# Attention weights times values in float32 on TensorE, with the output transposed, in place of a bf16 split on VectorE

## The chip, the cores and the metric

The kernel runs on all 8 NeuronCores of one Trainium2 chip, each core on its own half of one of four sequences, without exchange between the cores. The metric is the device time in microseconds of the slowest core. The median of two runs of the kernel before is 8694.8 us (8690.62 to 8698.98).

## What is computed

A layer normalisation and attention with 16 heads of 64, then a second layer normalisation and a feed-forward part with quantised weights, both with a residual addition. The change touches the attention alone:

```python
h = jnp.einsum('bse,end->bsnd', x, proj_weight)        # x after layer norm
q = jnp.einsum('bsnd,ndh->bsnh', h, attn_weight)
scores = jnp.einsum('bsnh,brnh->bsnr', q, h) / head_dim
w = jax.nn.softmax(scores, axis=-1)
v = jnp.einsum('brnd,ndh->brnh', h, value_weight)
attn_out = jnp.einsum('bsnr,brnh->bsnh', w, v).reshape(b, s, -1)
return attn_out @ out_w.T + out_b
```

Batch 4, 4096 positions, width 1024. A core holds one sequence of 4096 keys and computes 2048 of its queries.

## The kernel before

**Order of the work.** Every engine has one queue, written in the order of the `@blk` pieces, with semaphores between the queues; there is no scheduler. First the feed-forward weights are quantised (to about 600 us). Then, for each of two groups of four head pairs, `emit_hbuild` computes h for all 4096 positions (about 550 us each), and `emit_attention` runs once for each head pair (8 times, p = 0 to 7). The feed-forward part follows from about 5980 us on.

**float32 by halves.** Where float32 accuracy is wanted, a float32 tile is split into a bf16 tile "hi" and the bf16 rest "lo", and TensorE adds three bf16 products in PSUM: hi hi, hi lo, lo hi. Splitting takes VectorE a cast, a drain (it waits until its own writes are done) and a subtract.

**A head pair** (L554 to L873). Two heads of 64 lie in partitions 0 to 63 and 64 to 127. First the *value build* (L595 to L629): for 32 chunks of 128 keys (`NRC` = 32) TensorE computes v for both heads with six small matmuls, and VectorE writes it to `vA` and `vB` as 64 columns hi, a column of ones, and 64 columns lo. Then four *blocks* (`sc_i`) of 512 queries.

**A block.** TensorE computes the queries (L647), VectorE splits them and takes their largest absolute value (L658 to L661), a DMA issued by POOL brings that to one row (L669), and after some small steps a bias for the exponential lies in `cbias` (L707, semaphore `g_cb`).

The *loop* has 32 rounds over the key chunks (L737 to L755). In round rc TensorE issues the scores of the chunk, three matmuls of 512 columns for each head (L744, keys stationary, 64 rows of the array for each head), and after them the value matmuls of the chunk before (`emit_av`). ScalarE takes the exponentials of both heads into `w32`, float32, two slots for each head (L767). VectorE splits them into `w_hi` and `w_lo` (L777, L779). In `emit_av` the weights are stationary: for each head and each 128 queries a matmul of `w_hi` with 129 columns of v and one of `w_lo` with 65 (L720, L724), 16 in all. The column of ones gives the sum of the weights, so the result lies with queries on partitions and its sum beside it:

```python
te.matmul(pav[:, pofs:pofs + 129], w_hi[:, wofs + st * 128:wofs + (st + 1) * 128],
          vb[:, rc * 132:rc * 132 + 129], start=(rc == 0 and st % 2 == 0), stop=False)
```

The *tail*: VectorE takes eight reciprocals of the sums (L792), and for each head and 128 queries multiplies and adds the two parts (L801, L804). TensorE transposes the result (L817), VectorE splits it (L827, L829), TensorE multiplies it with the output weights (L848, 8 groups of three matmuls into `pb_q` and `pb_o` in turn), and VectorE adds each group to the residual `x_tm` (L872). The next block's query matmuls wait for the last of these additions (`v_res`), and its first score matmul for `g_cb`.

## Time and profile before

| | |
|---|---|
| profiled execution | 8699.6 us, span of the slowest core (2) 8698.0 us |
| spans of the 8 cores | 8682.4 to 8698.0 us |
| mean granted TensorE clock | 0.758 to 0.762 of full speed |
| TensorE matmuls busy | 4127.8 us, 47% of the span |
| VectorE busy | 5227.4 us, 60% |
| ScalarE busy | 1586.3 us, 18% |
| POOL busy | 67.7 us, 1% |

The profile is of one execution, so sums are made against its own 8699.6 us. A busy share is an average over stages; busy times of matmuls hold their latency, and matmuls overlap each other. A row of the timeline gives the start, the duration, engine, line and operation, output and inputs, and in brackets the idle time before it with the engine that ended it (DVEq and PEq are the sequencers of VectorE and TensorE, where a drain ends). "x2" are two instructions merged. The clock is a share of 2.4 GHz; 0.50 is 1.2 GHz.

### The profile page before, as it was taken

Reading aid. Unit: us, or ns where it says so; the run is one execution under the profiler, and the core shown is the slowest. Engines: PE = TensorE matmul, PEld = TensorE weight load, DVE = VectorE, ACT = ScalarE, POOL = GpSimd, SP = SyncE. Lnnn points to the kernel's source line nnn. Section 1 sums busy time; section 2 is a strip of 40 time slices with the busy share of each in tenths; the row PEclk is TensorE's granted clock in tenths of the full one; section 3 lists DMA queues with packets and bytes.
Section 4 is the critical chain, followed back from the end, with each engine's and each line's share of the span. In section 5 each row is a group of like instructions: output and inputs, shape, how many; then the busy total and the mean of one; then the engine's idle time right before and its main releaser. Section 6 shows DMA issues by size and latency. Waiting matters only on the chain.

```text
span 8698.0 us, 121004 instructions; the slowest of 8 cores (8682.4 to 8698.0 us)
## 1 busy us (share of the span) xinstructions
PE 4127.8 (47%) x38438; PEld 2597.9 (30%) x38438; DVE 5227.4 (60%) x12623; ACT 1586.3 (18%) x2602; POOL 67.7 (1%) x102
## 2 busy tenths in 40 slices
PE   0016645455555555645555454555454353353453
PEld 0015523223222225532222222323232232232232
DVE  5666667777677776667777777665434435434434
ACT  0000023233233331013233232321000000000000
POOL 0000000000000000000000000000000000000000
PEclk9996778788788887778888887876666665566666
DMA  8741000000000001100000000002333343343343
GB/s 271 234 137 35 30 6 1 4 1 1 4 1 1 1 9 41 35 11 1 4 1 1 4 1 1 1 1 47 75 87 66 75 90 67 67 99 66 78 85 70
DMA packets 835921, 394.33 MB, mean 45 GB/s; under 512 B 803427, under 2 KB 803555, under 8 KB 829156
## 3 DMA queue, kind: packets, MB, share of 16 engines
q1 hardware_dynamic: 827044, 353.00, 17.1%
q0 software_dynamic: 8256, 33.58, 1.0%
q8 instruction: 325, 5.32, 0.3%
q14 instruction: 296, 2.42, 0.1%
HBM read 352.95 MB, written 33.55 MB: 44 GB/s over the span
## 4 chain that ended last, share of the span: by engine, by line
DVE 47%; PE 26%; issue 12%; DMA 7%; DVEq 7%; ACT 1%; SPq 0%; ACTq 0%; POOLq 0%; POOL 0%
DVE w_lo L779 15%; DVE w_hi L777 9%; PE pb_av L462 6%; PE pf_d L1368 2%; PE pf_u L1195 2%; PE pf_g L1190 2%; PE pf_d L1195 2%; PE pf_d L1190 2%; DMA f_wd<-wdq 2%; PE pb_s L744 2%; DVE ln_lo L479 2%; DVE ln_hi L477 2%; PE pb_o L848 1%; DVE f_guq L1341 1%; PE pb_q L848 1%
## 5 line engine op out<-in xcount | busy, mean ns | idle before, releaser
L767 ACT ACTIVATE w<-pb_s,cbias 128x512 f32<-128x512 f32 x2048 | 1297.4, 684 | 1531.9 <-PE pb_s L744 1515.0
L779 DVE TENSOR_TENSOR w_lo<-w,w_hi 128x512 bf16<-128x512 f32 x2048 | 1417.9, 692 | 159.4 <-issue 6.8
L777 DVE CAST w_hi<-w 128x512 bf16<-128x512 f32 x2048 | 875.8, 428 | 561.2 <-issue 356.8
L720 PE MATMUL pb_av<-vA,w_hi 128*128 128x129 bf16 x4096 | 517.2, 226 | 1148.3 <-DVEq L782 1148.0
L720 PEld LDWEIGHTS pb_av<-vA,w_hi 128*128 128x128 bf16 x4096 | 384.0, 100 | 1646.7 <-issue 1646.7
L1368 PE MATMUL pf_d<-f_guq,f_wd 128*128 128x256 bf16 x2048 | 297.7, 319 | 634.4 <-DVE f_guq L1341 543.8
L720 PE MATMUL pb_av<-vB,w_hi 128*128 128x129 bf16 x4096 | 518.2, 226 | 0.0
L744 PE MATMUL pb_s<-q_hi,h_hi 64*128 64x512 bf16 x2048 | 461.4, 411 | 103.0 <-ACT w L767 72.1
L724 PE MATMUL pb_av<-vA,w_lo 128*128 128x65 bf16 x4096 | 491.9, 198 | 0.0
L724 PE MATMUL pb_av<-vB,w_lo 128*128 128x65 bf16 x4096 | 490.7, 198 | 0.0
L744 PE MATMUL pb_s<-q_lo,h_hi 64*128 64x512 bf16 x2048 | 455.9, 405 | 0.0
L744 PE MATMUL pb_s<-q_hi,h_lo 64*128 64x512 bf16 x2048 | 454.6, 404 | 0.0
L1368 PEld LDWEIGHTS pf_d<-f_guq,f_wd 128*128 128x128 bf16 x2048 | 230.5, 114 | 703.2 <-issue 645.3
L720 PEld LDWEIGHTS pb_av<-vB,w_hi 128*128 128x128 bf16 x4096 | 387.1, 101 | 0.0
L724 PEld LDWEIGHTS pb_av<-vB,w_lo 128*128 128x128 bf16 x4096 | 381.5, 100 | 0.0
L724 PEld LDWEIGHTS pb_av<-vA,w_lo 128*128 128x128 bf16 x4096 | 378.5, 100 | 0.0
L1190 PE MATMUL pf_g<-f_xqf,f_wg 128*128 128x256 bf16 x1024 | 202.8, 365 | 277.1 <-DVEq L1223 262.3
L1190 PE MATMUL pf_d<-f_xqf,f_wg 128*128 128x256 bf16 x1024 | 202.7, 364 | 273.8 <-DVEq L1223 273.8
L1233 ACT ACTIVATE f_si<-f_gr 128x256 f32<-128x256 f32 x256 | 106.6, 417 | 1232.2 <-DVEq L1223 1232.2
L462 PE MATMUL pb_av<-ln_hi,pw_hi 128*128 128x128 bf16 x2048 | 215.6, 268 | 239.8 <-DVE h_lo L492 234.2
L1210 DVE TENSOR_TENSOR f_gr<-pf_g,f_fb 128x256 f32<-128x256 f32 x128 | 54.4, 425 | 454.3 <-PE pf_u L1195 454.3
L1210 DVE TENSOR_TENSOR f_gr<-pf_d,f_fb 128x256 f32<-128x256 f32 x128 | 54.4, 425 | 452.0 <-PE pf_d L1195 448.1
(222 smaller groups left out, 6841.7 us busy)
## 6 DMA issues: line engine op xcount, KB each, us to landing
f_wg<-wgq SPq DMA_DIRECT2D x256, 256.0 KB, 3.3
f_wu<-wuq SPq DMA_DIRECT2D x256, 256.0 KB, 3.9
f_wd<-wdq SPq DMA_DIRECT2D x64, 1024.0 KB, 8.0
wraw<-wgT SPq DMA_DIRECT2D x16, 2048.0 KB, 10.2
wraw<-wuT SPq DMA_DIRECT2D x16, 2048.0 KB, 9.8
wraw<-wdT SPq DMA_DIRECT2D x64, 512.0 KB, 4.4
xa<-x_full SPq DMA_DIRECT2D x64, 512.0 KB, 3.5
x_tm<-x_full SPq DMA_DIRECT2D x16, 512.0 KB, 12.9
```

The lines of the kernel that those rows point to most:

```text
L462: last = te.matmul(pp[:, 0:128], wop[:, ic * 512 + lc * 128:ic * 512 + (lc + 1) * 128], rop[:, ic * 128:(ic + 1) * 128], start=first, stop ...
L477: v.tensor_copy(ln_hi[:, ib * 128:(ib + 1) * 128], src)
L479: v_ls.inc(v.tensor_tensor(ln_lo[:, ib * 128:(ib + 1) * 128], src, ln_hi[:, ib * 128:(ib + 1) * 128], ALU.subtract))
L720: te.matmul(pav[:, pofs:pofs + 129], w_hi[:, wofs + st * 128:wofs + (st + 1) * 128], vb[:, rc * 132:rc * 132 + 129], start=(rc == 0 and st ...
L724: last = te.matmul(pav[:, pofs:pofs + 65], w_lo[:, wofs + st * 128:wofs + (st + 1) * 128], vb[:, rc * 132:rc * 132 + 65], start=False, sto ...
L744: last = te.matmul(pb_s[hidx][:, 0:512], kop[hidx * 64:hidx * 64 + 64, hofs + rc * 128:hofs + (rc + 1) * 128], qop[hidx * 64:hidx * 64 + 6 ...
L767: a_e.inc(sc.activation(w32[:, slot:slot + 512], pb_s[hidx][:, 0:512], AFT.Exp, bias=cbias[:, hidx:hidx + 1], scale=1.0 / 64))
L777: v.tensor_copy(w_hi[:, slot:slot + 512], w32[:, slot:slot + 512])
L779: v.tensor_tensor(w_lo[:, slot:slot + 512], w32[:, slot:slot + 512], w_hi[:, slot:slot + 512], ALU.subtract)
L1190: te.matmul(pg[:, 0:FSC], f_wg[:, buf + ic * 128:buf + (ic + 1) * 128], f_xqf[:, ic * FSC:(ic + 1) * FSC], start=(ic == 0), stop=(ic == 7))
L1195: last = te.matmul(pu[:, 0:FSC], f_wu[:, buf + ic * 128:buf + (ic + 1) * 128], f_xqf[:, ic * FSC:(ic + 1) * FSC], start=(ic == 0), stop=(i ...
L1368: last = te.matmul(pd[:, 0:FSC], f_wd[:, (ec % 2) * 4096 + ic * 128:(ec % 2) * 4096 + (ic + 1) * 128], f_guq[:, ic * FSC:(ic + 1) * FSC], ...
```

## The change

The weights are no longer split. The value matmul is turned round: v is stationary (float32, 64 columns and the column of ones, so 65) and the float32 weights are the moving operand, 512 queries at once. There is one matmul for each head and round, waiting for ScalarE itself (`a_e`). Its output has the head's 64 dimensions on partitions 0 to 63 and the sums in row 64, queries along the free axis. This form is the one the output projection wants, so the transposes go; but the sums now lie in one row, so their reciprocals are taken as rows of 512, split into hi and lo, and spread over the partitions by one-row matmuls with a row of ones into `pb_av[0]` and `pb_av[1]`. The second head's result lies in partitions 0 to 63 and is moved to 64 to 127 by a DMA that POOL issues. The projection writes to `pb_av[0]` and `pb_av[1]` instead of `pb_q` and `pb_o`, so the next block's query matmuls wait for `g_cb` instead of `v_res`, and the first score matmul waits no longer for `g_cb`. ScalarE waits for the value matmuls two rounds back instead of VectorE's split. `vA` and `vB` become float32 tiles of 66 columns for each chunk, written by a copy and a memset.

```diff
+                        v.tensor_copy(vb[:, rc * 66:rc * 66 + 64], pav[:, 0:64])
+                        v.memset(vb[:, rc * 66 + 64:rc * 66 + 65], 1.0)
-                        v.tensor_copy(vb[:, rc * 132:rc * 132 + 64], pav[:, 0:64])
-                        v.memset(vb[:, rc * 132 + 64:rc * 132 + 65], 1.0)
-                        v.drain()
-                        v.tensor_tensor(vb[:, rc * 132 + 65:rc * 132 + 129],
-                                        pav[:, 0:64],
-                                        vb[:, rc * 132:rc * 132 + 64], ALU.subtract)
                     v_ve.inc(v.drain())
...
                     v_ve.w(te, bvve + NRC)
                     t_s.w(te)
-                    v_res.w(te)
+                    g_cb.w(te)
...
                     def emit_av(rc):
-                        v_w.w(te, bvw + 2 * rc + 2)
                         for hidx in range(2):
+                            a_e.w(te, bae + 2 * rc + hidx + 1)
+                            if rc == 0:
+                                v_af.w(te, bvaf)
                             wofs = (2 * (rc % 2) + hidx) * 512
                             vb = [vA, vB][hidx]
-                            last = None
-                            for st in range(4):
...
+                            last = te.matmul(
+                                pb_av[2 + hidx][0:65, 0:512],
+                                vb[:, rc * 66:rc * 66 + 65],
+                                w32[:, wofs:wofs + 512],
+                                start=(rc == 0), stop=(rc == NRC - 1))
                         t_av.inc(last)
 
-                    g_cb.w(te, bgcb + 1)
-                    v_nm.w(te, bvnm)
-                    v_af.w(te, bvaf)
+                    a_e.w(te, bae)
...
                     t_av.w(v, btav + NRC)
                     t_at.w(v, btat)
                     for hidx in range(2):
...
+                        v.reciprocal(rr_t[64:65, hidx * 512:(hidx + 1) * 512],
+                                     pb_av[2 + hidx][64:65, 0:512])
                     v.drain()
...
+                    for hidx in range(2):
+                        te.matmul(pb_av[hidx][:, 0:512],
+                                  onesb_t[64:65, 0:128],
+                                  rhib[64:65, hidx * 1024:hidx * 1024 + 512],
+                                  start=True, stop=False, tile_position=(64, 0))
+                        t_at.inc(te.matmul(
...
+                    v.tensor_copy(fbA_t[:], pb_av[0][:, 0:512])
...
+                    v.tensor_tensor(attn_tm[0:64, 0:512], pb_av[2][0:64, 0:512],
+                                    fbA_t[0:64, 0:512], ALU.mult)
...
+                @blk.gpsimd
+                def _(gp):
+                    v_af.w(gp, bvaf + 4)
+                    d_pk.inc(gp.dma_start(out=attn_tm[64:128, 0:512],
+                                          in_=attnB_s[0:64, 0:512]), 16)
+
+                @blk.vector
+                def _(v):
+                    d_pk.w(v)
+                    v.tensor_copy(attn_hi[:], attn_tm[:])
+                    v.drain()
+                    v.tensor_tensor(attn_lo[:], attn_tm[:], attn_hi[:], ALU.subtract)
+                    v_as.inc(v.drain())
...
-                            pp = [pb_q, pb_o][eh]
+                            pp = [pb_av[0], pb_av[1]][eh]
```

TensorE in the loop, before, from the last score matmul of a round on. `pb_av` is the accumulator, `vA` the values of the first head, `w_hi` and `w_lo` the halves of the weights:

```order
L744 MATMUL pb_s<-q_hi,h_lo 128x512
L720 MATMUL pb_av<-vA,w_hi 128x129 [waits v_w]
L724 MATMUL pb_av<-vA,w_lo 128x65
L720 MATMUL pb_av<-vA,w_hi 128x129
L724 MATMUL pb_av<-vA,w_lo 128x65
```

The pair of rows L720 and L724 stands eight times in a row, four times for each head, behind one wait for VectorE. The same place after the change (line numbers of the changed kernel):

```order
L735 MATMUL pb_s<-q_hi,h_lo 128x512
L718 MATMUL pb_av<-w,vA 65x512 [waits a_e]
L718 MATMUL pb_av<-w,vB 65x512 [waits a_e]
L735 MATMUL pb_s<-q_hi,h_hi 128x512 [waits a_e]
L735 MATMUL pb_s<-q_lo,h_hi 128x512
L735 MATMUL pb_s<-q_hi,h_lo 128x512
```

Two instructions have taken the place of sixteen, each waits for ScalarE alone, and the order of scores and values is the same.

VectorE from the end of a loop to the residual, before:

```order
L779 TENSOR_TENSOR w_lo<-w,w_hi 128x512
L784 UNCONDITIONAL_BRANCH
L792 RECIPROCAL sums_t<-pb_av 128x1 [waits t_av]
L792 RECIPROCAL sums_t<-pb_av 128x1 x7
L801 TENSOR_SCALAR attn_tm<-pb_av,sums_t 128x64
L804 SCALAR_TENSOR_TENSOR attn_tm<-pb_av,sums_t,attn_tm 128x64
```

The last two rows stand eight times; then come four casts and subtracts of 128 columns, each pair behind a transpose. After the change, from behind the reciprocals on:

```order
L772 CAST rhib<-rr_t 1x512 x2
L776 TENSOR_TENSOR rhib<-rr_t,rhib 1x512 x2
L797 UNCONDITIONAL_BRANCH
L801 COPY fbA_t<-pb_av 128x512 [waits t_at]
L804 COPY fbB_t<-pb_av 128x512 [waits t_at]
L806 TENSOR_TENSOR attn_tm<-pb_av,fbA_t 64x512
L809 TENSOR_TENSOR attnB_s<-pb_av,fbB_t 64x512
L819 UNCONDITIONAL_BRANCH
L822 CAST attn_hi<-attn_tm 128x512 [waits d_pk]
L824 TENSOR_TENSOR attn_lo<-attn_tm,attn_hi 128x512
```

`fbA_t` and `fbB_t` hold the spread reciprocals, `d_pk` is the new DMA. The piece has fewer and longer instructions, and waits once for TensorE's spreading and once for the DMA. The split of `attn_tm` and the projection behind it now wait for all 512 queries, where before each 128 went on by themselves.

## Rows read from the trace of the kernel before

**Rows 1.** Timeline of VectorE (DVE), a round of the loop.

```profile
4003.15 0.43 DVE L777 CAST w_hi<-w 128x512 bf16<-128x512 f32 x1 [0.19 <-issue]
4003.65 0.69 DVE L779 TENSOR_TENSOR w_lo<-w,w_hi 128x512 bf16<-128x512 f32 x1
...
4005.91 0.43 DVE L777 CAST w_hi<-w 128x512 bf16<-128x512 f32 x1 [0.18 <-issue]
```

**Rows 2.** Timeline of TensorE (PE), the same round.

```profile
4002.55 0.40 PE L744 MATMUL pb_s<-q_hi,h_hi 64*128 64x512 bf16 x2
...
4002.77 0.39 PE L744 MATMUL pb_s<-q_lo,h_hi 64*128 64x512 bf16 x2
...
4004.52 0.22 PE L720 MATMUL pb_av<-vA,w_hi 128*128 128x129 bf16 x1 [1.14 <-DVEq L782]
...
4005.18 0.19 PE L724 MATMUL pb_av<-vB,w_lo 128*128 128x65 bf16 x1
...
4005.30 0.40 PE L744 MATMUL pb_s<-q_hi,h_hi 64*128 64x512 bf16 x2
```

**Rows 3.** Timeline of ScalarE (ACT), the same round.

```profile
4003.52 1.26 ACT L767 ACTIVATE w<-pb_s,cbias 128x512 f32<-128x512 f32 x2 [1.50 <-PE pb_s L744]
```

**Rows 4.** Stretches: length, busy us and count of PE, PEld, DVE, ACT, POOL, clock, DMA, GB/s.

```profile
3960.20:3970.00 9.80, 6.87 (x46) 3.05 (x47) 4.48 (x8) 4.22 (x6) 0.00 (x0) 0.52 0.00 0
...
3976.50:4055.00 78.50, 45.11 (x619) 27.07 (x617) 62.72 (x112) 35.11 (x56) 0.00 (x0) 1.00 0.01 1
...
684.00:689.00 5.00, 3.92 (x48) 3.29 (x45) 2.42 (x7) 0.29 (x1) 0.00 (x0) 0.81 0.40 105
```

**Rows 5.** Timeline of VectorE, the first reciprocals of three blocks in a row.

```profile
3932.57 0.62 DVE L792 RECIPROCAL sums_t<-pb_av 128x1 f32<-128x1 f32 x8 [1.28 <-PE pb_av L724]
...
4055.97 0.63 DVE L792 RECIPROCAL sums_t<-pb_av 128x1 f32<-128x1 f32 x8 [1.53 <-PE pb_av L724]
...
4178.43 0.62 DVE L792 RECIPROCAL sums_t<-pb_av 128x1 f32<-128x1 f32 x8 [1.33 <-PE pb_av L724]
```

**Rows 6.** Timeline of TensorE, first projection matmul, first scores, round 1, next block.

```profile
3941.83 0.63 PE L848 MATMUL pb_q<-ow_hi,attn_hi 128*128 128x512 bf16 x1
...
3960.18 0.61 PE L744 MATMUL pb_s<-q_hi,h_hi 64*128 64x512 bf16 x2 [0.97 <-DVE cbias L707]
...
3965.26 0.63 PE L744 MATMUL pb_s<-q_hi,h_lo 64*128 64x512 bf16 x1
...
4083.46 0.61 PE L744 MATMUL pb_s<-q_hi,h_hi 64*128 64x512 bf16 x2 [0.97 <-DVE cbias L707]
```

**Rows 7.** Timeline of TensorE, float32 transposes of 128 columns in the h build.

```profile
3303.22 0.27 PE L447 MATMUL pb_o<-id32s,lnt 128*128 128x128 f32 x1
3303.32 0.38 PE L447 MATMUL pb_s<-id32s,lnt 128*128 128x128 f32 x2
```

**Rows 8.** Groups of instructions by line: count, busy us, mean ns, idle before.

```profile
L872 DVE TENSOR_TENSOR x_tm<-x_tm,pb_o 128x512 f32<-128x512 f32 x128 | 88.1, 689 | 63.8 <-PE pb_o L848 36.7 <-PE pb_o L857 26.6 <-issue 0.5
...
L1281 DVE RECIPROCAL f_trw<-f_trw 1x256 f32<-1x256 f32 x8 | 13.9, 1741 | 0.7 <-issue 0.2
```

**Rows 9.** Timeline of VectorE, behind the small DMA of POOL.

```profile
3957.00 0.21 DVE L675 TENSOR_REDUCE csc<-mq_row 1x1 f32<-1x64 f32 x1 [2.72 <-DMA mq_row<-mq_t]
```

**Rows 10.** DMA issues: count, KB each, median us from issue to landing.

```profile
y<-x_tm POOLq DMA_DIRECT2D x16, 512.0 KB, 3.3
...
mq_row<-mq_t POOLq DMA_DIRECT2D x32, 0.5 KB, 1.9
```

**Rows 11.** Timeline of VectorE, one key chunk of the value build.

```profile
4345.92 0.23 DVE L623 CAST vA<-pb_av 128x64 bf16<-128x64 f32 x1 [0.19 <-issue]
...
4346.37 0.21 DVE L623 CAST vB<-pb_av 128x64 bf16<-128x64 f32 x1
...
4347.08 0.23 DVE L623 CAST vA<-pb_av 128x64 bf16<-128x64 f32 x1 [0.18 <-issue]
```

**Rows 12.** Timeline of VectorE, first step of a block's queries.

```profile
3952.22 0.69 DVE L658 CAST q_hi<-pb_q 128x512 bf16<-128x512 f32 x1 [1.20 <-PE pb_q L647]
```

More of the change, by code:

```diff
@@ L146, in _ @@
         v.memset(ones_row[:], 1.0)
+        v.memset(onesb_t[:], 1.0)
         v.memset(sc_t[:, 0:1], 0.75)
@@ L772, in _ @@
                 def _(v):
-                    for rc in range(NRC):
-                        for hidx in range(2):
-                            a_e.w(v, bae + 2 * rc + hidx + 1)
-                            slot = (2 * (rc % 2) + hidx) * 512
-                            v.tensor_copy(w_hi[:, slot:slot + 512], w32[:, slot:slot + 512])
-                            v.drain()
-                            v.tensor_tensor(w_lo[:, slot:slot + 512],
-                                            w32[:, slot:slot + 512],
-                                            w_hi[:, slot:slot + 512], ALU.subtract)
-                            v_w.inc(v.drain())
-                @blk.vector
-                def _(v):
                     t_av.w(v, btav + NRC)
@@ L811, in _ @@
                     v_nm.w(te, bvnm + 1)
-                    a_e.w(te, bae + 64)
-                    for st in range(4):
-                        tid = btat + st
-                        if st >= 2:
-                            v_af.w(te, bvaf + st - 1)
-                        t_at.inc(te.transpose(
-                            pb_s[st % 2][:, 0:128],
-                            attn_tm[:, st * 128:(st + 1) * 128], id32[:]))
+                    v_res.w(te, bvres)
+                    for hidx in range(2):
+                        te.matmul(pb_av[hidx][:, 0:512],
+                                  onesb_t[64:65, 0:128],
+                                  rhib[64:65, hidx * 1024:hidx * 1024 + 512],
+                                  start=True, stop=False, tile_position=(64, 0))
+                        t_at.inc(te.matmul(
+                            pb_av[hidx][:, 0:512],
+                            onesb_t[64:65, 0:128],
+                            rhib[64:65, hidx * 1024 + 512:hidx * 1024 + 1024],
+                            start=False, stop=True, tile_position=(64, 0)))
@@ L821, in _ @@
                 @blk.vector
                 def _(v):
+                    t_at.w(v, btat + 1)
                     t_op.w(v, btop)
-                    for st in range(4):
-                        t_at.w(v, btat + st + 1)
-                        src = pb_s[st % 2][:, 0:128]
-                        v.tensor_copy(attn_hi[:, st * 128:(st + 1) * 128], src)
-                        v.drain()
-                        v_af.inc(v.tensor_tensor(
-                            attn_lo[:, st * 128:(st + 1) * 128], src,
-                            attn_hi[:, st * 128:(st + 1) * 128], ALU.subtract))
+                    v.tensor_copy(fbA_t[:], pb_av[0][:, 0:512])
```

86 lines of the change are left out of this document (39 added, 47 removed).

## The prediction

> **What bounds the kernel now.** I read the granted clock of all cores first (0.758 to 0.762, spans within 16 us, so one core stands for all), then the busy time in 100 us stretches, which showed where the 32 attention blocks lie, then the timeline of one block, engine by engine. A block is 512 query rows of one head pair: a loop of 32 rounds over the keys, and a tail that normalises, projects and adds.
>
> In the loop VectorE sets the pace. From one CAST of the first head to the next is 4005.91 - 4003.15 = 2.76 us [rows 1], and it spends them on two casts (0.43) and two subtracts (0.69), each started by a semaphore. TensorE's score matmuls start 0.22 us apart, and the two heads go side by side (x2) [rows 2]: 3 x 0.215 = 0.65 us a round. The 16 value matmuls take 0.66 us (4004.52 to 5.18), and before them TensorE idles 1.14 us for VectorE's drain. ScalarE does two exponentials in 1.26 us and idles 1.50 [rows 3]. So nothing but the split of the weights into two bf16 halves holds a round at 2.76.
>
> The whole loop, from the first score matmul to the first reciprocal, takes 4055.97 - 3960.18 = 95.8 us in one block and 4178.43 - 4083.46 = 95.0 in the next [rows 5, 6]. I use 95. The way from that reciprocal to the output projection is 3941.83 - 3932.57 = 9.3 us, and to the next loop 27.6 us; here work goes from engine to engine one step at a time. In the loop proper TensorE is granted 1.00 (2.4 GHz), in its first 10 us 0.52, which is almost all at 1.2 GHz [rows 4].
>
> **The loop after.** The VectorE split goes. TensorE takes the float32 weights as moving operand, in two matmuls of 512 columns a round. What an ordinary float32 matmul costs is not in the trace, since all float32 ones there are transposes. Low bound: the rate of bf16, 0.215 us per 512 columns [rows 2]. The float32 transposes stand about 0.11 us apart for 128 columns [rows 7], so 0.44 per 512. High bound: four products, each at that transpose rate, 1.74. Between them I take four products at the bf16 rate, 4 x 0.215 = 0.86 us: this kernel itself builds a nearly float32 product of three bf16 products (it leaves out low times low), and the nearest matmuls with 512 columns are those score matmuls. The other end of the transposes, 0.44, would be two products and is a rival below.
>
> The Trainium skill (FP8 and Floating Point Precision, TensorE Precision Notes) says that a true float32 product is four passes through the array; by it the price of a matmul would be the same 0.86 us, and no run before this one shows it.
>
> A round is then 0.65 + 2 x 0.86 = 2.37, and I add 0.07 us at each change between score and value matmuls: from the last value matmul to the next score matmul 0.12 us pass (4005.18 to 5.30), of which its 65 columns are about 0.03 [rows 2]. That gives 2.50 us, with TensorE busy without a gap. It is the bound if the exponentials keep up: they start 0.97 us after the first score matmul and are done at 2.23 (4002.55, 4003.52 + 1.26) [rows 2, 3], and their word reaches TensorE some 0.14 later, at 2.37. The value matmuls of the round before are only done at about 2.43. So the cover is thin, 0.06 us, and whatever makes the value matmuls cheaper brings little below 2.4 unless the heads stagger.
>
> The start of a loop is at half clock. The last score matmul of round 1 starts 5.1 us after the first of round 0 [rows 6], ends its columns at 5.5, and then a pair of value matmuls costs 3.4 us: 8.9; scores of round 2 end at 10.2. Here the clock comes up [rows 4], and the second pair ends at about 12.0. Thirty rounds remain: 30 x 2.50 = 75.0, and 0.4 for the last drain and semaphore. Loop: 87.4 us, **-7.6 us x 32 = -243**.
>
> **The tail after.** On VectorE two reciprocals of 1 x 512 stand where eight of 128 x 1 stood. The only long reciprocal in the trace takes 1741 ns for 256 elements [rows 8], so 3.4 us each, 6.8. (If it cost as much as any operation of 512 elements, 0.69 [rows 8], the block would be 5.4 us shorter, 173 us in all. That is the low bound.) Two casts of 0.43 and two subtracts of 0.69 with drains: 9.2 us after the first reciprocal. Then TensorE's four one-row matmuls at half clock, 0.43 to the second and 0.63 for it [rows 6], with a semaphore: the first factor is there at 10.5. Two copies and two products on VectorE, 0.69 and a drain each: 13.6. The DMA through POOL moves 128 KB between partitions. A tiny one keeps VectorE waiting 2.72 us [rows 9], 1.9 of it from issue to landing, where 512 KB take 3.3 [rows 10]. So 0.8 us are the way to the issue, and with 2.15 for the landing I take 2.95; bounds 2.7 and 0.8 + 3.3 = 4.1 (1.15 x 32 = 37 us more). At 16.6 VectorE casts and subtracts 512 columns, 17.9, and the projection starts at 18.2 instead of 9.3: +8.9. The projection and the residual additions stay, only in other PSUM banks. What is queued behind the new DMA wait on VectorE is the residual, and behind TensorE's wait the projection: nothing can fill the gap.
>
> Two waits get lighter. The first score matmul no longer waits for the bias copy, of which 0.97 us are seen [rows 6]; about 0.85 come back, hidden by nothing, because the exponential table is loaded only after the scores. Sum per block 8.9 - 0.85 = 8.05, **x 32 = +258**. The query matmul no longer waits for the last residual addition, since the projection has left its bank: VectorE idles 1.20 us for it [rows 12], 1.1 come back in the 24 blocks that have another block of the same pair before them, **-26**.
>
> **The value build.** Per key chunk VectorE did cast, memset, drain, subtract for each head, 4347.08 - 4345.92 = 1.16 us, at half clock and with TensorE ahead of it. Without the drain and subtract a head goes from 0.45 (4345.92 to 6.37) to about 0.24: 0.66 in all with the 0.18 of semaphore [rows 11]. -0.5 us x 32 chunks x 8 pairs = **-128**. Bounds: 0 if the ping-pong with TensorE takes over, -150 at best.
>
> **Sum** against the profiled execution's 8699.6 us: -243 + 258 - 26 - 128 = -139, 8561. The median of the shown runs is 4.8 us lower, so **8557 us**, 1.6% less. The change wins in the loop, pays it back in the tail, and what stays is the value build. I give this case its own range of 8470 to 8650, a round of 2.42 to 2.60 being 30 x 32 x 0.18 = 173 us of it.
>
> **Rival 1, the clock (slower).** TensorE goes from half idle to streaming all of the loop, on eight cores. In the stretch at 684 us, in a phase of dense matmuls, the granted clock is 0.81 [rows 4], while the loops show 1.00 with TensorE idle 1.14 of 2.76 us. If the loops run at 0.81, the streaming part 2.37 becomes 2.91 and a round 3.05; the loop is 12.6 + 91.5 + 0.2 = 104.3, +9.3 x 32 = +298 instead of -243, so 9098 us. It decides once the loop gains less than the (258 - 154)/32 = 3.2 us a block that the rest loses: 91.8 us, a round of (91.8 - 12.4)/30 = 2.65, which a mean clock of 0.94 already brings (2.37/0.94 + 0.14). For it: the 0.81 was granted to matmuls that paused between rounds. Against it: value matmuls with 65 of 128 columns leave half of the array unused.
>
> The Trainium skill (TensorE: Matmul & The Clock Gate, Part 1) warns of a limiter that takes a die to 13/16 of the clock within about 5 to 20 us once a third core of it runs dense matmuls. By that rule all loops here would run at 0.81, which is this rival's 9098 us; the trace agrees only in that a grant of 0.81 exists.
>
> **Rival 2, dearer float32.** At 1.74 a matmul a round is 4.27 and the time near 10350 us; a weight load left uncovered ahead of each of the eight products, some 0.07 us, gives 3.06 and 9100. For it: float32 transposes run at half the bf16 rate. Against: bf16 loads are fully covered in the loop.
>
> **Rival 3, cheaper float32.** With two products, 0.44 a matmul, the exponentials bind: the heads stagger, six score matmuls in a row and 0.87 of values, about 2.25 with changes. Loop 79.5, -15.5 x 32 = -496, 8304 us.
>
> **Chances.** Forecast 0.47, rival 1 0.30, rival 2 0.12, rival 3 0.11. Faster by over 2% (under 8521, about what a measurement can tell from no change): all of rival 3 and 0.14 of the forecast, 0.25. Slower by over 2%: rivals 1 and 2, 0.42. Within: 0.33. The range, 8300 to 9150, leaves out the dear end of rival 2, the low edge of rival 3 and a little of rival 1.
>
> **What would show it.** Right: two value matmuls a round, their passes about 0.215 us apart, round 2.50 with TensorE never idle for a releaser; first reciprocal to projection 18 us, half of it reciprocals; value chunks 0.66 apart. Wrong: granted clock under 1.00 late in the loop (rival 1), passes dearer than 0.215 at full clock (2), a round under 2.4 with TensorE waiting for ACT (3), or a reciprocal row far from 3.4 us.

## The result and the profile after

The changed kernel takes 8582.8 us (median) against 8700.0 us of the kernel before in the same session. The ratio is 0.9865, with a 95% interval of 0.9852 to 0.9879: 1.35% faster, which is inside the 2% that I called no change, and 26 us from the 8557 us of the prediction. The profiled execution took 8585.86 us, 113.7 less than the 8699.6 of the one before. In three of the nine executions of this kernel one die or both show a lower mean clock and the time is 8773 to 8877 us, which is longer than the kernel before took in any; such executions (of some variants up to 6% longer) are left out of every comparison here.

The page of the kernel after, busy times and one of the costliest groups (line, engine, operation, output and inputs, count, busy time and mean, idle time before and what ended it):

```profile
span 8584.3 us, 85041 instructions; the slowest of 8 cores (8553.9 to 8584.3 us)
PE 5086.0 (59%) x26150; PEld 2252.7 (26%) x26150; DVE 2983.5 (35%) x7376; ACT 1588.9 (19%) x2602; POOL 83.1 (1%) x134
...
L768 DVE RECIPROCAL rr_t<-pb_av 1x512 f32<-1x512 f32 x64 | 210.1, 3320 | 2848.3 <-PE pb_av L718 2848.3
```

VectorE's busy time falls from 5227.4 to 2983.5 us and its idle time now stands ahead of the reciprocals: it does nothing in the loops. TensorE's rises from 4127.8 to 5086.0. That 2244 us of VectorE work are gone and 114 us of time is the first thing to take from this page: the work that went lay partly beside TensorE's, and TensorE's own grew into the room.

TensorE in one round at full clock, core 1 (start, duration, operation; x2 is one for each head), answering to [rows 2]:

```profile
2230.04 0.40 PE L735 MATMUL pb_s<-q_hi,h_hi 64*128 64x512 bf16 x2
...
2230.49 0.39 PE L735 MATMUL pb_s<-q_hi,h_lo 64*128 64x512 bf16 x2
2230.80 1.07 PE L718 MATMUL pb_av<-w,vA 128*65 128x512 f32 x2
2231.71 1.02 PE L718 MATMUL pb_av<-w,vB 128*65 128x512 f32 x2
2232.66 0.40 PE L735 MATMUL pb_s<-q_hi,h_hi 64*128 64x512 bf16 x2
```

No row has an idle time in brackets. The round is 2232.66 - 2230.04 = 2.62 us, and so it is in every block. For the scores x2 is one matmul for each head; a float32 matmul shows as two records, so there x2 is one head. Taken singly, inside one kind of matmul, the records stand 0.429 us apart, so a float32 matmul of 512 columns takes 0.858 us, four times 0.215. The ends of a round are dearer than I had them. Last score start to first value start is 2230.80 - 2230.49 = 0.31, where the columns of the score matmul are 0.215: 0.10 for the change. Behind the last value matmul 2231.71 + 2 x 0.43 would be 2232.57, and the next score matmul starts at 2232.66: 0.10 again. Head A takes 2231.71 - 2230.80 = 0.91, 0.05 over 0.86. So 0.65 + 1.72 + 0.25 = 2.62.

The stretch at full clock (busy us of PE, PEld, DVE, ACT, POOL, each with its count, then granted clock, DMA share, GB/s), and ScalarE in the round, answering to [rows 4] and [rows 3]:

```profile
2190.00:2270.00 80.00, 80.00 (x304) 21.21 (x303) 0.00 (x0) 38.06 (x60) 0.00 (x0) 1.00 0.00 1
```

```profile
2231.01 1.27 ACT L759 ACTIVATE w<-pb_s,cbias 128x512 f32<-128x512 f32 x2 [1.35 <-PE pb_s L735]
```

TensorE is busy for 80 of 80 us at a granted clock of 1.00. The exponentials are done at 2232.28, 0.38 us before TensorE's next score matmul; 0.14 of that is the way of their word, which leaves 0.24. Up to the end of the value matmuls' columns at 2232.57 the cover is 0.15, where I had priced 0.06.

The start of a block:

```profile
2305.14 0.62 PE L735 MATMUL pb_s<-q_hi,h_hi 64*128 64x512 bf16 x2
...
2310.78 1.93 PE L718 MATMUL pb_av<-w,vA 128*65 128x512 f32 x2
2312.55 1.02 PE L718 MATMUL pb_av<-w,vB 128*65 128x512 f32 x2
2313.50 0.40 PE L735 MATMUL pb_s<-q_hi,h_hi 64*128 64x512 bf16 x2
```

Head A's float32 matmul takes 1.77 us (at half clock), head B's 0.95: the clock came up inside the first pair of value matmuls, on the mean of the 32 blocks 8.2 us after the first score matmul, where before it was 10.75. In this execution the loops of all eight cores show 0.50 at the start and 1.00 from then on, and no other level.

VectorE in the tail, answering to [rows 5] and [rows 8], and TensorE's two releases in it:

```profile
2394.13 6.57 DVE L768 RECIPROCAL rr_t<-pb_av 1x512 f32<-1x512 f32 x2 [88.59 <-PE pb_av L718]
2400.77 0.75 DVE L772 CAST rhib<-rr_t 1x512 bf16<-1x512 f32 x2
...
2404.70 0.69 DVE L801 COPY fbA_t<-pb_av 128x512 f32<-128x512 f32 x1 [1.46 <-PE pb_av L791]
...
2407.19 0.68 DVE L809 TENSOR_TENSOR attnB_s<-pb_av,fbB_t 64x512 f32<-64x512 f32 x1
2410.80 0.43 DVE L822 CAST attn_hi<-attn_tm 128x512 bf16<-128x512 f32 x1 [2.92 <-DMA attn_tm<-attnB_s]
```

```profile
2412.28 0.59 PE L843 MATMUL pb_av<-ow_hi,attn_hi 128*128 128x512 bf16 x1 [6.90 <-DVEq L825]
```

From the first reciprocal to the projection 2412.28 - 2394.13 = 18.15 us, with the two long pieces where the prediction put them: 6.6 of reciprocals and 2.92 of waiting for the DMA.

The value build, one chunk 2160.85 - 2160.28 = 0.57 us where it was 1.16 [rows 11]:

```profile
2160.28 0.23 DVE L626 COPY vA<-pb_av 128x64 f32<-128x64 f32 x1 [0.19 <-PE pb_av L612]
...
2160.85 0.23 DVE L626 COPY vA<-pb_av 128x64 f32<-128x64 f32 x1 [0.19 <-PE pb_av L612]
```

Means over the blocks of each trace, in us, x being how often the stretch occurs:

| | before | after | difference | x | sum | predicted |
|---|---|---|---|---|---|---|
| first score matmul to first reciprocal | 95.23 | 89.39 | -5.84 | 32 | -186.6 | -243 |
| first reciprocal to projection | 9.02 | 17.83 | +8.81 | 32 | +282.2 | +285 |
| split of the queries to first score matmul | 7.95 | 7.12 | -0.83 | 32 | -26.5 | -27 |
| last residual to next query split, in a pair (1.89 and 0.85 in most) | 2.00 | 0.92 | -1.08 | 24 | -25.9 | -26 |
| the same with the value build between | 44.63 | 25.04 | -19.6 | 6 | -117.6 | -96 |
| start of the program to the first query split | 1157.2 | 1139.7 | -17.5 | 1 | -17.5 | -16 |
| last residual to query split, with the h build between | 584.4 | 566.8 | -17.6 | 1 | -17.6 | -16 |
| projection and residual additions | 9.87 | 9.57 | -0.30 | 32 | -9.6 | 0 |
| behind the last block | 2734.7 | 2740.1 | +5.4 | 1 | +5.4 | 0 |

Each of the eight value builds lies in one of the three rows that name a build or the start: together -153 us, predicted -128. The sum of all rows is -113.7 us, as the two spans of 8698.0 and 8584.3 us have it.

### The profile page after: what moved, and what is told of

It is laid out like the page before. It is cut to its first block, busy times and chain, and to the rows that moved or that the text cites. A ratio compares the mean times of both kernels' runs of the same rounds, so it can differ in the third digit from the quotient of the medians.

```text
span 8584.3 us, 85041 instructions; the slowest of 8 cores (8553.9 to 8584.3 us)
## 1 busy us (share of the span) xinstructions
PE 5086.0 (59%) x26150; PEld 2252.7 (26%) x26150; DVE 2983.5 (35%) x7376; ACT 1588.9 (19%) x2602; POOL 83.1 (1%) x134
## 3 DMA queue, kind: packets, MB, share of 16 engines
q1 hardware_dynamic: 827044, 353.00, 17.6%
## 4 chain that ended last, share of the span: by engine, by line
PE 55%; DVE 23%; DMA 8%; issue 7%; DVEq 6%; ACT 0%; SPq 0%; POOLq 0%; ACTq 0%; POOL 0%
PE pb_av L718 23%; PE pb_s L735 10%; PE pb_av L464 6%; PE pb_av L843 3%; PE pf_d L1364 2%; PE pf_u L1191 2%; PE pf_g L1186 2%; PE pf_d L1191 2%; PE pf_d L1186 2%; DMA f_wd<-wdq 2%; DVE ln_lo L481 2%; DVE ln_hi L479 2%; DVE f_guq L1337 1%; DVE f_gr L1328 1%; DVE rr_t L768 1%
## 5 line engine op out<-in xcount | busy, mean ns | idle before, releaser
L768 DVE RECIPROCAL rr_t<-pb_av 1x512 f32<-1x512 f32 x64 | 210.1, 3320 | 2848.3 <-PE pb_av L718 2848.3
L718 PE MATMUL pb_av<-w,vA 128*65 128x512 f32 x2048 | 1125.2, 632 | 0.0
L718 PE MATMUL pb_av<-w,vB 128*65 128x512 f32 x2048 | 1055.4, 597 | 0.0
L718 PEld LDWEIGHTS pb_av<-w,vB 128*65 128x65 f32 x2048 | 287.2, 140 | 617.6 <-issue 617.6
L735 PEld LDWEIGHTS pb_s<-q_hi,h_hi 64*128 64x128 bf16 x2048 | 109.4, 93 | 888.3 <-issue 886.0
L718 PEld LDWEIGHTS pb_av<-w,vA 128*65 128x65 f32 x2048 | 203.4, 138 | 454.1 <-issue 454.1
L843 PE MATMUL pb_av<-ow_hi,attn_hi 128*128 128x512 bf16 x256 | 124.3, 486 | 232.8 <-DVEq L825 221.5
L464 PEld LDWEIGHTS pb_av<-ln_hi,pw_hi 128*128 128x128 bf16 x2048 | 178.1, 125 | 253.4 <-issue 253.4
L1191 PE MATMUL pf_u<-f_xqf,f_wu 128*128 128x256 bf16 x1024 | 232.8, 404 | 0.0
L867 DVE TENSOR_TENSOR x_tm<-x_tm,pb_av 128x512 f32<-128x512 f32 x256 | 176.3, 689 | 160.9 <-PE pb_av L843 101.1
```

Source lines behind the costliest of these rows:

```text
L464: last = te.matmul(pp[:, 0:128], wop[:, ic * 512 + lc * 128:ic * 512 + (lc + 1) * 128], rop[:, ic * 128:(ic + 1) * 128], start=first, stop ...
L718: last = te.matmul(pb_av[2 + hidx][0:65, 0:512], vb[:, rc * 66:rc * 66 + 65], w32[:, wofs:wofs + 512], start=(rc == 0), stop=(rc == NRC - 1))
L735: last = te.matmul(pb_s[hidx][:, 0:512], kop[hidx * 64:hidx * 64 + 64, hofs + rc * 128:hofs + (rc + 1) * 128], qop[hidx * 64:hidx * 64 + 6 ...
L768: v.reciprocal(rr_t[64:65, hidx * 512:(hidx + 1) * 512], pb_av[2 + hidx][64:65, 0:512])
L843: last = te.matmul(pp[:, 0:512], a[:, st * 128:(st + 1) * 128], o[:, eh * 512:(eh + 1) * 512], start=first, stop=stop)
L867: v_res.inc(v.tensor_tensor(xd, xd, pp[:, 0:512], ALU.add))
```

## The experiments

My theory went on record with each run: the loop is bound by TensorE's streaming, four passes to a float32 matmul and a price for each change between the two kinds of matmul; the tail is a chain in which reciprocals and DMA are paid in full. The rivals: the clock, the exponentials, and the orientation of the product as the true cause.

**e_stat: the weights stay the stationary operand, in float32.** This undoes the transposed output and the new tail, and keeps the missing split.

```diff
-                            last = te.matmul(
-                                pb_av[2 + hidx][0:65, 0:512],
-                                vb[:, rc * 66:rc * 66 + 65],
-                                w32[:, wofs:wofs + 512],
+                            for st in range(4):
+                                last = te.matmul(
+                                    pb_av[2 * hidx + st // 2][
+                                        :, (st % 2) * 129:(st % 2) * 129 + 65],
+                                    w32[:, wofs + st * 128:wofs + (st + 1) * 128],
+                                    vb[:, rc * 66:rc * 66 + 65],
...
-                        v.reciprocal(rr_t[64:65, hidx * 512:(hidx + 1) * 512],
-                                     pb_av[2 + hidx][64:65, 0:512])
+                            v.reciprocal(sums_t[:, 4 * hidx + st:4 * hidx + st + 1],
+                                         pav[:, pofs + 64:pofs + 65])
```

> The changed kernel, but the float32 weights are the stationary operand again (128x128) and the float32 values the moving one (65 columns), with the old tail (reciprocals of 128x1, one multiply each, transposes, no spreading, no DMA). Theory A, the weight load sets the price: the float32 loads of 65 columns took 0.13 to 0.14 us in the changed kernel and are covered by passes of 0.43; loads of 128 columns cannot be covered by passes of 65 columns, so two loads a matmul of 0.11 to 0.14 us make 1.7 to 2.2 us a round for eight matmuls against 1.72 now; round 2.6 to 3.1. Theory B, only the streamed columns count: four passes of 65 columns are 0.11 us a matmul, 0.87 a round, and the exponentials bind at about 2.2. Both: the tail from the first reciprocal to the projection falls from 17.8 to about 6.5 us (9.0 of the kernel before, less eight operations of 0.36), -360 us in 32 blocks. Time: A 8220 to 8720, B about 7800 us.

Measured: 10533.5 us, ratio 1.2108 (1.2090 to 1.2126). TensorE's matmuls and its weight loads in one round, and a stretch of the loop:

```profile
3101.82 1.97 PE L719 MATMUL pb_av<-vA,w 128*128 128x65 f32 x8
3103.58 1.91 PE L719 MATMUL pb_av<-vB,w 128*128 128x65 f32 x8
3105.42 0.62 PE L738 MATMUL pb_s<-q_hi,h_hi 64*128 64x512 bf16 x2
```

```profile
3101.81 1.78 PEld L719 LDWEIGHTS pb_av<-vA,w 128*128 128x128 f32 x8 [0.84 <-issue]
```

```profile
3100.00:3150.00 50.00, 50.00 (x222) 37.79 (x221) 0.00 (x0) 12.64 (x20) 0.00 (x0) 0.50 0.00 1
```

The granted clock is 0.50 through every loop: it never rises, in none of the 32, on none of the eight cores. The eight value matmuls are 16 records, 0.213 us apart (with the changes at both ends 3105.42 - 3101.82 = 3.60 us), in two equal parts: a load starts, the matmul starts 0.106 us behind it, and the next load 0.107 us behind that. At 1.2 GHz the 130 columns of two passes are 0.108 us, and the load takes about the same; nothing of it is covered. The round is 5.01 us, the loop 163.1, +73.7 x 32 = +2360; the old tail is back (4.81 us to the projection), -417. Together +1943, and the profiled executions differ by +1953. Theory A had the load right (0.107 us, expected 0.11 to 0.14) and the clock wrong, so neither of the two times, 7800 and up to 8720 us, came near.

What follows: with weights stationary half of TensorE's time in a value product is loading. The Trainium skill (TensorE: Matmul & The Clock Gate, Weight-path perf modes) says that the fast weight load works for 128 columns and not for float32; the trace agrees, the load taking as long as the 130 columns that follow it. The same matmuls in bf16 (the run e_stat_bf1 below), at the same 1.2 GHz, start 0.054 us apart, which is their 65 columns alone:

```profile
2300.05 0.40 PE L719 MATMUL pb_av<-vA,w 128*128 128x65 bf16 x4
2300.26 0.41 PE L719 MATMUL pb_av<-vB,w 128*128 128x65 bf16 x4
```

By my estimate the round of e_stat would at 2.4 GHz be half of 5.01, 2.5 us, no worse than the 2.62 of the changed kernel. So the uncovered loads alone do not make this kernel slow; the clock that did not rise does. Why it stays down here, with TensorE shown busy in all of the stretch, no run settles.

**e_nodma: VectorE writes head B's product to partitions 64 to 127 itself,** and the DMA and its wait go.

```diff
-                    v.tensor_tensor(attnB_s[0:64, 0:512], pb_av[3][0:64, 0:512],
+                    v.tensor_tensor(attn_tm[64:128, 0:512], pb_av[3][0:64, 0:512],
...
-                    d_pk.inc(gp.dma_start(out=attn_tm[64:128, 0:512],
-                                          in_=attnB_s[0:64, 0:512]), 16)
...
-                    d_pk.w(v)
```

> The changed kernel, but VectorE writes the second head's product straight to partitions 64 to 127, so the DMA through POOL and its wait go. Theory, the tail is a chain with nothing beside it: first reciprocal to projection falls from 17.8 by the 2.95 us that I gave the DMA to 14.9, 32 times, -94 us: 8492. Rival: part of the DMA was hidden, or a write that changes the partitions is slower than 0.69 us: under 50 us less.

Measured: 8504.7 to 8512.9 us, ratio 0.9783 (0.9763 to 0.9802). VectorE, core 3:

```profile
2381.36 0.68 DVE L809 TENSOR_TENSOR attn_tm<-pb_av,fbB_t 64x512 f32<-64x512 f32 x1
2382.16 0.43 DVE L815 CAST attn_hi<-attn_tm 128x512 bf16<-128x512 f32 x1
```

The product that shifts partitions takes 0.68 us like the other, and the cast follows 0.80 after it, where in the changed kernel it stood 3.61 later (2407.19 to 2410.80). First reciprocal to projection 15.02 instead of 17.83, -2.81 x 32 = -90. Some of that is given back elsewhere in the block (loop +0.15, projection and residual +0.26), and the profiled executions differ by 81. The DMA wait was on the path in full, and needless.

**e_norecip: a copy in place of each reciprocal.** The softmax's division is left out.

```diff
-                        v.reciprocal(rr_t[64:65, hidx * 512:(hidx + 1) * 512],
+                        v.tensor_copy(rr_t[64:65, hidx * 512:(hidx + 1) * 512],
```

> The changed kernel with the two reciprocals of 1x512 replaced by copies of the same form, so the result is not divided by the sums. Theory: a copy takes 0.43 to 0.69 us in place of 3.32, so 5.3 to 5.8 us less in each tail, -168 to -185 us: about 8410. Rival: the time of such a row lies in reading one partition of PSUM, not in the reciprocal, and the copies take as long: no change, 8586.

Measured: 8425.9 us, ratio 0.9685 (0.9666 to 0.9704), so 157 us less than after. Core 0:

```profile
2348.36 1.29 DVE L768 COPY rr_t<-pb_av 1x512 f32<-1x512 f32 x2 [89.59 <-PE pb_av L718]
```

Two copies take 1.29 us, two reciprocals 6.57. First reciprocal to projection is 12.26, -5.57 x 32 = -178. The loop is 0.26 longer and the projection chain 0.35, together +19: what follows a shorter pause is not quite the same afterwards. So the two rows of 512 sums cost 5.3 us a block more than copies of the same form, and this is the largest part of what the transposed output did to the tail.

**e_bf1: weights and values in bf16, without low parts.** Same instructions, other types, so the value matmul is one pass and not four.

```diff
-        vA = asb("vA", [128, NRC * 66], F32)
-        vB = asb("vB", [128, NRC * 66], F32)
+        vA = asb("vA", [128, NRC * 66], BF16)
+        vB = asb("vB", [128, NRC * 66], BF16)
...
-                     bsb("w32", [128, 4 * 512], F32),
+                     bsb("w32", [128, 4 * 512], BF16),
```

> The changed kernel with bf16 weights (written so by ScalarE) and bf16 values, so the low parts are left out and a value matmul is one pass of 0.215 us. Theory of the prediction, the four passes are the bound and below about 2.4 us the exponentials bind with the heads staggered: round about 2.25, -0.37 x 1024 = -380 us, 8205 us, TensorE waiting for ACT. Rival: the heads stagger so well that a round is only the chain of one head (score 0.82, exponential 0.69, two semaphores of 0.15, 1.8 us): 7750 us. Second rival: the gaps between score and value matmuls (0.25 us a round now) come from float32 alone and vanish here.

Measured: 7772.8 us, ratio 0.8934 (0.8917 to 0.8952). TensorE, core 7 (each head alone now, x1):

```profile
2199.94 0.37 PE L735 MATMUL pb_s<-q_hi,h_hi 64*128 64x512 bf16 x1
...
2200.52 0.37 PE L735 MATMUL pb_s<-q_hi,h_hi 64*128 64x512 bf16 x1
...
2200.95 0.37 PE L735 MATMUL pb_s<-q_hi,h_lo 64*128 64x512 bf16 x1
2201.25 0.41 PE L718 MATMUL pb_av<-w,vA 128*65 128x512 bf16 x1
2201.49 0.38 PE L718 MATMUL pb_av<-w,vB 128*65 128x512 bf16 x1
2201.80 0.39 PE L735 MATMUL pb_s<-q_hi,h_hi 64*128 64x512 bf16 x1
...
2202.31 0.37 PE L735 MATMUL pb_s<-q_hi,h_hi 64*128 64x512 bf16 x1
```

ScalarE in the same round:

```profile
2200.90 1.27 ACT L759 ACTIVATE w<-pb_s,cbias 128x512 bf16<-128x512 f32 x2 [0.52 <-PE pb_s L735]
2202.78 1.26 ACT L759 ACTIVATE w<-pb_s,cbias 128x512 bf16<-128x512 f32 x2 [0.61 <-PE pb_s L735]
```

This round is 2202.78 - 2200.90 = 1.88 us, the mean at full clock 1.84, and the loop is 63.7 instead of 89.4. My theory, a round of 2.25 and 8205 us, fails, and the first rival, 7750 us, is nearly met. Two things are read here. First, the heads stagger: head B's scores start 0.58 after head A's, not beside them. Its next ones start at 2202.31, 0.14 after its exponential is done (2200.90 + 1.27 = 2202.17), so a head's own chain of scores, exponential and word back now sets when it may go on. TensorE's columns and changes, one behind the other, would be 6 x 0.215 + 2 x 0.215 + 0.18 = 1.90, a little more than the mean because head B's first score matmul starts 0.15 behind head A's last, and the run does not part the two bounds. Second, the changes are still there with bf16 values: 2201.25 - 2200.95 = 0.30 and 2201.80 - 2201.49 = 0.31, each 0.09 over the 0.215 of the columns. The price belongs to the switch between score matmuls (64 rows of the array for each head) and value matmuls (all 128), not to float32; only 0.05 of the 0.25 us is float32's. That it is the number of rows, and not something else in which the two kinds differ, is not shown by a run of its own. Six passes less should give 1.29 us, and 0.78 came: the pairing of the heads' scores, worth up to 0.65, is mostly lost.

The Trainium skill (TensorEngine Tiling (Array Packing), Key Properties) says that a change of tiling mode drains TensorE. The trace agrees in that each change between 64 and 128 rows costs 0.09 to 0.10 us.

**e_pair: two rounds of scores, then two rounds of values.** It halves the number of changes and leaves the matmuls as they are. The spare banks of PSUM take the second round's scores. With the order go eight weight slots, waits of the loop that reach back one or two rounds further, and one more wait ahead of the first score matmul, for the last residual addition.

```diff
+            def sbank(rc, hidx):
+                return pb_s[hidx] if rc % 2 == 0 else pb_av[hidx]
...
-                        if rc >= 1:
-                            emit_av(rc - 1)
+                        if rc >= 2 and rc % 2:
+                            emit_av(rc - 3)
+                            emit_av(rc - 2)
...
-                     bsb("w32", [128, 4 * 512], F32),
+                     bsb("w32", [128, 8 * 512], F32),
```

> The changed kernel with two rounds taken together: scores of chunks 2k and 2k+1 (the second into the PSUM banks that are free in the loop), then the value matmuls of 2k-2 and 2k-1, with eight weight slots. Theory: 0.25 us of each round of 2.62 are the two changes between matmuls on 64 rows and on 128 rows (0.10 before and 0.10 behind the value matmuls, and 0.05 in the first), and not waits; with half the changes a round is 2.49 to 2.50, -0.125 x 1024 = -128 us, 8458 us. Rival: the gap is the wait for the exponentials, whose end leaves 0.06 us of cover; then the round falls to the streaming time, 2.37, -256 us, 8330. Second rival: gap with every instruction that waits on a semaphore, whose number stays: 2.62, 8586.

Measured: 8450.7 and 8467.9 us, ratio 0.9725 (0.9704 to 0.9746). TensorE, core 2:

```profile
2309.00 0.40 PE L739 MATMUL pb_s<-q_hi,h_hi 64*128 64x512 bf16 x2
...
2313.99 0.40 PE L739 MATMUL pb_s<-q_hi,h_hi 64*128 64x512 bf16 x2
```

Two rounds take 2313.99 - 2309.00 = 4.99 us where two rounds of after take 5.24: one pair of changes, 0.25, is gone. The loop is 84.71 us, -4.68 x 32 = -150, of which the rest of the block gives back about 0.5 us each. Neither rival's round, 2.37 or 2.62, fits the 2.49 measured, so the change between the kinds is confirmed as the term that I had undersized.

**e_waits: the two waits of before, put back.**

The first line stands ahead of the query matmul, the second ahead of the first score matmul.

```diff
+                    v_res.w(te)
...
+                    g_cb.w(te, bgcb + 1)
```

> The changed kernel with the two old waits put back: the query matmuls wait for the last residual addition, and the first score matmul for the bias copy. Theory: both lay on the path, so 0.85 x 32 + 1.05 x 24 = 52 us come back, 8638 us, and the rows show 7.95 instead of 7.12 us from the query cast to the first score and 1.9 instead of 0.85 from the residual to the query cast. Rival: the exponential's table load, 1.28 us, hides the first: 25 us only.

Measured: 8661.7 to 8673.2 us, ratio 0.9965 (0.9946 to 0.9984). The waits show, core 5:

```profile
2325.41 0.41 PE L648 MATMUL pb_q<-h_hi,aw_hi 64*64 64x512 bf16 x2 [1.05 <-DVE x_tm L869]
...
2334.29 0.62 PE L737 MATMUL pb_s<-q_hi,h_hi 64*128 64x512 bf16 x2 [0.86 <-DVE cbias L708]
```

1.04 x 24 and 0.86 x 32 come back, 52 us, as priced. The profiled execution is 83 us slower than after's, though. The rest stands in the loop (90.14 against 89.39, +0.75 x 32 = 24) and behind it (+0.25 x 32 = 8), and the clock rises 9.8 us after the first score matmul instead of 8.2. So 52 us of waits cost 83. The two kernels differ in nothing but the waits, so the later rise comes from them; by what means, no run shows.

**e_stat_bf1: weights stationary, in bf16 without low parts.** The diff is that of e_stat and that of e_bf1 together. It asks whether float32 or the orientation keeps the clock down.

> Weights stationary as in the run before the last four, but weights and values in bf16 (the low parts left out), so loads are the fast ones of 0.1 us. It asks why the float32 form with stationary weights stayed at 1.2 GHz for the whole loop. Theory A, TensorE was granted the low clock because it spent its time on loads and streamed little; bf16 with stationary weights streams even fewer columns in its value matmuls (8 x 65), but the scores fill more of a shorter round, so the clock comes up, the round is 1.87 as with moving bf16 weights, the tail 4.8 in place of 17.8: 7773 - 416 = 7357 us. Theory B, stationary weights of this shape keep the clock low whatever their type: scores at half clock with the heads staggered, round 2.8 to 3, time about 8400 us.

Measured: 7533.0 us, ratio 0.8660 (0.8635 to 0.8685). Two stretches of one loop, core 4:

```profile
2294.50:2340.00 45.50, 43.04 (x239) 16.52 (x239) 0.22 (x2) 23.31 (x36) 0.00 (x0) 0.50 0.00 1
2345.00:2365.00 20.00, 19.39 (x158) 8.16 (x156) 0.00 (x0) 14.02 (x23) 0.00 (x0) 1.00 0.01 2
```

The clock comes up here, but on the mean 35 us after the first score matmul, from 12.6 to 79.8 in single blocks, and in one of the 32 not at all; the loop is 63.2 to 81.7 us accordingly. So the orientation alone does not keep the clock down: with bf16 the rise comes late, and with float32 it does not come. Theory A has the loop too short for that reason, and theory B fails. The mean loop is 69.7 us, 6 longer than e_bf1's, and the old tail pays for it and more: from the first reciprocal to the end of the last residual addition it is 15.2 us against e_bf1's 28.3, -13.1 x 32 = -419. It is 240 us faster than e_bf1 in all.

**b_stat: e_stat_bf1 with the pairing of e_pair.** A candidate to beat both kernels, with the low parts of weights and values left out. Its diff is the three above; the output of one head is four groups of 65 columns in one bank, and `w32` is bf16 with 8 slots.

> A candidate: bf16 weights and values (low parts left out), weights stationary with one accumulator bank a head, the old tail with one multiply for each piece, and two rounds taken together with double score banks. Theory: with two rounds of scores ahead the chain of one head's exponential no longer binds, ScalarE does: 2 x 0.63 = 1.27 us a round, 1.3 with the changes, 0.57 x 1024 = 584 us less than with the rounds single: about 6780 us if the clock comes up. Rival: at half clock scores 1.28, value matmuls at least 8 x 0.1 and the changes 0.3 make 2.4 us a round: 7900 us.

Measured: 6708.4 us, ratio 0.7714 (0.7702 to 0.7726). A stretch of a loop at full clock, and the reciprocals behind it, core 7:

```profile
1798.00:1830.00 32.00, 32.00 (x373) 16.80 (x371) 0.00 (x0) 30.12 (x52) 0.00 (x0) 1.00 0.01 2
```

```profile
1833.72 0.63 DVE L777 RECIPROCAL sums_t<-pb_av 128x1 f32<-128x1 f32 x8 [43.11 <-PE pb_av L722]
```

The 52 exponentials in the 32 us are 26 rounds, 1.23 us each. ScalarE is busy for 30.1 of the 32 us, so it is near its bound. TensorE is shown busy in all of them, but that holds the latency of its matmuls: the starts and changes are by my estimate 0.65 + 8 x 0.03 + 0.09 = 0.98 us of the 1.23. The loop is 43.75 us (the clock rises after 7.7 on the mean, in six of the loops of this core to 0.81 for a part, which cost 1 to 2 us each) and the tail to the projection 4.79, so -45.64 x 32 - 13.04 x 32 = -1878 against after; the profiled executions differ by -1864. Eight reciprocals of 128 x 1 take 0.63 us where two of 1 x 512 take 6.57. The late rise of e_stat_bf1 is not repeated, though the value matmuls are the same: this kernel differs from it in the order of the rounds, with its slots and waits, and in the banks alone. It is the fastest of all kernels here by far, as long as bf16 weights are enough for the use.

**b_pair: e_pair and e_nodma together,** the candidate that keeps float32.

> The changed kernel, float32 throughout, with the two edits that gained by themselves: VectorE writes the second head's product to the upper partitions (no DMA, -74 us measured), and two rounds are taken together (-125 us measured). Theory: loop and tail are one chain, so gains in them add up: 8586 - 74 - 125 = 8387 us. Rival: a shorter tail makes the clock come up at another place in the loop and eats part of it, as the run with the old waits lost more (83) than its waits (52): 8410 to 8450.

Measured: inconclusive. One execution took 8362.9 us, five others 8709 to 8900 (the kernel before, beside them, 8699 to 8709 in seven), and no ratio can be given. The profile is of one of the five:

```profile
core 3: 8772.3 us, clock 0.717
...
core 7: 8340.6 us, clock 0.768
die 0 (median of its cores): 8763.2 us, clock 0.717
die 1 (median of its cores): 8334.1 us, clock 0.768
```

The same stretch on core 3 and on core 7:

```profile
2263.50:2298.80 35.30, 34.80 (x116) 10.30 (x117) 0.00 (x0) 16.54 (x28) 0.00 (x0) 0.81 0.00 1
```

```profile
2263.50:2298.80 35.30, 35.30 (x148) 11.07 (x144) 0.00 (x0) 16.95 (x28) 0.00 (x0) 1.00 0.00 1
```

On die 0 TensorE is granted 0.81 in the loop, at the same place in the same work for which die 1 gets 1.00, and its cores end 429 us later. Die 1, at 8334, and the one execution agree with the sum of the two edits (8586 - 135 - 81 = 8370). So the float32 version with both edits is the fastest of them where the full clock is granted, which was one execution in six; in the other five it was no faster than the kernel before. What decides which comes, no run shows.

## Why the prediction was right, and where it was off

- **The bound of the loop: right.** TensorE streams without a gap for a releaser, and a float32 matmul is 0.858 us, predicted 0.86. The Trainium skill's four passes (FP8 and Floating Point Precision, TensorE Precision Notes) are what the trace shows, with 4 x 0.215. Rival 2, dearer float32, falls for this orientation. Its uncovered weight load is seen in the other one: in e_stat each load costs 0.107 us at 1.2 GHz.
- **The round: right in kind, mis-sized in a term.** "I add 0.07 us at each change between score and value matmuls" was read from one gap behind a value matmul of before, and read low: 0.12 less the 0.03 of the columns is 0.09. It is 0.10 each, and 0.05 more for the first float32 matmul: 0.25 a round and not 0.14, so 2.62 and not 2.50, 30 x 0.12 x 32 = +115 us. e_pair takes half of the changes away and gains 150 us in the loops. The measured 2.62 lies outside the 2.42 to 2.60 that I gave for this case, and only 0.03 under the 2.65 at which, by the prediction's own working, the change would have lost.
- **The start of the loop: too dear.** The clock rises at 8.2 us and not at 10. The loop is 89.4 and not 87.4; by the longer round alone it would be 91.0, so the start gives back 1.6 x 32 = -52 us, which I did not foresee. Another -7 come from the loops of before, 95.23 on the mean where I used 95.
- **The tail: right to 0.1 us** (+8.81 on the mean, predicted +8.9). Reciprocals 3.32 each, predicted 3.4; the wait for the DMA 2.92, predicted 2.95. Both ends of the sum were 0.3 to 0.4 us high (9.3 for 9.02, 18.2 for 17.83), which cancels. That "half of it" would be reciprocals was a slip: by the prediction's own 6.8 of 18.2 it is over a third, as measured. e_norecip and e_nodma show both in full on the path, 178 and 90 us.
- **The two waits: right in themselves** (-27 and -26), but putting them back costs about 30 us more, most of it through the loop, which I had not in the sum. Their worth is rather -83 than -52; the table books the rest under the loop.
- **The value build: undersized.** A chunk is 0.57 and not 0.66, so -0.59 x 256 = -151, and -153 by the table, just beyond the "-150 at best". The wait of 0.19 is still there, so the two heads take 0.38 us and not the 0.48 that I had.
- **Rival 1, the clock at 0.81,** had 0.30. In the profiled execution of after no loop of any core shows it. It exists: all four cores of die 0 had it in b_pair, in 25 to 27 of their 32 loops, and in b_stat cores of both dies had it in up to six loops. What keeps the compared executions of after free of it, no run shows. The Trainium skill's limiter (TensorE: Matmul & The Clock Gate, Part 1) would hold a die at 13/16 whenever three cores run dense matmuls; here eight cores stream all of the loop at 1.00 in one execution and one die at 0.81 in another, so the trace agrees on the level and, in b_pair, on the die as the unit, and not that it always comes.
- **Rival 3's floor of 2.25** needed cheap matmuls, and e_bf1 had them: its own formula (six score matmuls in a row, the value passes and two changes) gives 1.90 with one pass a head, measured 1.84 on the mean. With float32 the cover of the exponentials was 0.15 and not 0.06 us, because the dearer changes let the value matmuls end later. The claim in the forecast that cheaper value matmuls "brings little below 2.4 unless the heads stagger" ended in its last four words: they stagger.

The errors are +115 (changes), -52 (start of the loop), -7 (base), -25 (value build), -3 (tail), +1 (the two waits) and -4 (projection and what lies behind the last block), which is +25: from the predicted -139 to the measured -114. The median lies 3.1 us under the profiled execution where I had set 4.8, and that makes the 26 us between 8557 and 8582.8. The sum is closer than its terms, and that is luck: an error of 115 us is hidden by the others.

## What to carry to other kernels

Turning a product round so that one engine is relieved moves the layout of everything behind it: here the sums went from a column on 128 partitions (0.63 us for all the reciprocals of a block) to two rows of one partition (6.57 us), and the tail with its longer chain ate the gain of the loop (+282 against -187 us). Price such a tail by the longest row and not by the number of elements, and look for the version that keeps the layout. Where TensorE is full, count the changes between tile shapes and group what has one shape. And where weights and values may be rounded to bf16, leave the low parts out first: that is worth 810 us by itself (e_bf1), and the old orientation and the pairing then give 1064 more, down to 6708 us, where in float32 the pairing gave 135 and the old orientation lost 1953.

## What of the hardware was not expected

- A change between matmuls on 64 rows and on 128 rows costs 0.09 to 0.10 us each way, with float32 and with bf16 values.
- With float32 stationary operands the granted clock stayed at 1.2 GHz in all 32 loops of 163 us on all eight cores, while the trace shows TensorE busy without a pause. With bf16 ones of 128 x 128 it rose 35 us into the loop on the mean, with paired rounds of the same matmuls 7.7 us into it. What decides, no run here shows.
- VectorE reads partitions 0 to 63 and writes 64 to 127 in 0.68 us, as without the shift.
- A reciprocal costs 6.5 ns for each element of a row (3320 ns for 512) where a copy takes 0.64 us for the row.
- With waits of 1.04 and 0.86 us ahead of the loop the clock rose 1.6 us later after the loop's start, and the loop was 0.75 us longer.
